# Step sizes of a state-space layer computed in two halves: eight token tiles inside the norm stage ahead of it, eight inside its scan, and a reordered opening of the scan

## The reference, cut to what matters

```python
h = rmsnorm(hidden_states, norm_w)
z, xBC, dt = split(h @ in_proj_w.T)            # 256, 512 and 4 columns
xBC = silu(causal_conv(xBC, 4 taps) + conv_b); x, B, C = split(xBC)
dt = softplus(dt + dt_bias)                    # one step size for each token and head
dA = exp(dt * -exp(A_log))                     # its decay
h_t = h_{t-1} * dA_t + dt_t * B_t x_t          # scan over the tokens, 4 heads
y_t = C_t . h_t + D * x_t;  y = rmsnorm(y * silu(z), w) @ out_proj_w.T
```

## Time and profile before

| | us |
|---|---|
| median of 3 runs (1836.56 to 1837.46) | 1837.18 |
| the profiled execution, whole | 1835.85 |
| its span, from first to last instruction | 1834.1 |
| the state-space stage, first TensorE work to the next stage's | 1427.89 to 1559.38 |
| of it the opening, to the first `scores` | 1427.89 to 1464.30 |

### The profile page before, as it was taken

How to read it: one execution, slowest core, us unless ns; L and a number is a source line. 1 busy time by engine, 2 the same in 40 slices (tenths; PEclk the granted TensorE clock), 3 DMA queues, 4 the chain that set the end, 5 groups by cost and what they waited for, 6 DMA issues and landing times. The chain is left out here.

```text
span 1834.1 us, 25946 instructions
## 1 busy us (share of the span) xinstructions
PE 1683.9 (92%) x10028; PEld 795.2 (43%) x10028; DVE 1263.6 (69%) x1804; ACT 1194.6 (65%) x2436; POOL 182.9 (10%) x171
## 2 busy tenths in 40 slices
PE   6999999999999999749999999999886699699997
PEld 3433333333333333235444444455554466344443
DVE  4888888888888887046888677675375276255555
ACT  4588888888888888735677777777546564333332
POOL 1000000000000000130000000111245000100100
PEclk9899999999999999979899999999988799699999
DMA  1000000000000000010000000000100000212220
GB/s 61 1 1 1 1 1 1 1 1 1 1 1 1 1 1 1 20 28 1 1 1 1 1 1 1 1 1 2 36 1 0 12 1 1 106 60 93 98 84 26
DMA packets 7274, 29.98 MB, mean 16 GB/s; under 512 B 680, under 2 KB 2736, under 8 KB 4848
## 3 DMA queue, kind: packets, MB, share of 16 engines
q1 hardware_dynamic: 7152, 28.33, 4.2%
HBM read 27.15 MB, written 1.18 MB: 15 GB/s over the span
## 5 line engine op out<-in xcount | busy, mean ns | idle before, releaser
L879 DVE TENSOR_REDUCE a_part_max<-a_ps 128x2 f32<-128x1024 f32 x512 | 602.3, 1220 | 87.1 <-PE a_ps L681 86.5
L864 ACT ACTIVATE a_probs<-a_ps 128x512 f32<-128x512 f32 x1024 | 533.2, 613 | 131.0 <-PE a_ps L777 128.6
L879 DVE TENSOR_REDUCE f_part_max<-f_ps 128x2 f32<-128x1024 f32 (+3 forms) x320 | 327.7, 1061 | 121.3 <-PE f_ps L681 65.3
L777 PE MATMUL a_ps<-a_q_shift,a_KA 64*128 64x512 f32 x1024 | 367.7, 448 | 3.8 <-POOL a_q_shift L660 2.6
L864 ACT ACTIVATE f_probs<-f_ps 128x512 f32<-128x512 f32 (+3 forms) x640 | 300.2, 538 | 99.8 <-PE f_ps L781 48.6
L777 PEld LDWEIGHTS a_ps<-a_q_shift,a_KA 64*128 64x128 f32 x1024 | 166.4, 187 | 291.4 <-ACT a_probs L864 275.5
L681 PE MATMUL a_ps<-a_KA,a_q_open 64*128 64x512 f32 x1024 | 277.7, 468 | 4.4 <-DVE a_part_max L879 3.7
L795 PE MATMUL a_psO<-a_probs,a_VA 128*32 128x512 f32 x2048 | 275.6, 610 | 3.9 <-ACT a_probs L864 3.9
L777 PE MATMUL f_ps<-f_q_shift,f_KA 64*128 64x512 f32 (+3 forms) x640 | 224.1, 435 | 4.8 <-POOL f_q_shift L660 2.2
L681 PE MATMUL f_ps<-f_KA,f_q_open 64*128 64x512 f32 (+3 forms) x640 | 170.3, 430 | 5.2 <-DVE f_part_max L879 4.4
L777 PEld LDWEIGHTS f_ps<-f_q_shift,f_KA 64*128 64x128 f32 x640 | 106.3, 188 | 150.2 <-ACT f_probs L864 138.5
(11 more groups left out here) (321 smaller groups left out, 1780.3 us busy)
## 6 DMA issues: line engine op xcount, KB each, us to landing
t_c_all<-c_rows SPq DMA_DIRECT2D x16, 1024.0 KB, 8.0
experts_w<-in_experts SPq DMA_DIRECT2D x1, 3264.0 KB, 10.3
W<-in_weights SPq DMA_DIRECT2D x1, 1574.0 KB, 6.3
out<-X SPq DMA_DIRECT2D x4, 256.0 KB, 6.9
K<-in_consts SPq DMA_DIRECT2D x1, 644.0 KB, 7.0
R<-in_rows SPq DMA_DIRECT2D x1, 530.0 KB, 6.0
W<-in_weights SPq DMA_DIRECT2D x1, 512.0 KB, 6.8
mx_conv_rows<-in_conv_rows SPq DMA_DIRECT2D x1, 512.0 KB, 4.1
```

The source lines that it names most:

```text
L777: mm = pe.matmul(bank(r)[:, lo:512], g.KA[rows, 2 * n + jp, P * s:P * s + P], q_shift[rows, u % 2, jp, lo:512], start=True, stop=not diag)
L864: nc.scalar.activation(probs[:, st % 2, j, lo:512], bank(r)[:, lo:512], ACT.Exp, scale=SCALE).then_inc(ring_read, 1)
L879: dve.tensor_reduce(part_max[:, 4 * q + 2 * jp:4 * q + 2 * jp + 2, c], ps1[:, k % 2, :, 0:b - a], AX_X, ALU.max).then_inc(max_read, 1)
```

## The change

A class `StepSizes` now holds the whole calculation for eight tiles. It is used twice. The first use (`u_`, tiles 0 to 7) is written into the norm stage: `logits` on TensorE after its last `add_scaled`, `sums` between the two last `turn_u`; on VectorE `raw` after the last `mixture`, `one_more` and `step_size` ahead of `stats3(3)`; on ScalarE `exp_raw` and `log` around `apply2(3)`, and `decays` ahead of the last block. There, `scale_u`, the part of `apply3` that makes `U`, is split off and put ahead of `apply3` for the two last blocks. The second use (`mx_`, tiles 8 to 15) is written into the scan: `logits` at chunk 1, `sums` at chunk 5; `raw`, `one_more`, `step_size` at chunks 1, 2, 3; `exp_raw` and `log` in ScalarE's part for block 1, `decays` in that for block 2. `dt`, `a`, `decay` and `Aneg` are now allocated outside the two stages. In the opening, `decays_of(0)` comes ahead of the convolutions, `spread_a(0)` is ScalarE's first work, `exponent(0)` follows the pad copies, and `spread_a(1)` and `(2)` stand ahead of the Silu work.

The diff, cut to its core (`...` marks what is left out):

```diff
+class StepSizes:
...
+    def logits(self, pe, bank):
+        for t in range(8):
+            at = CONV - 1 + P * (self.first + t)
+            mm = pe.matmul(bank[:, MH * t:MH * t + MH], g.UT[:, at:at + P], g.w("mzdt")[:, DI:DI + MH], start=True, stop=True)
...
+    def log(self, act):
+
+        act.wait_ge(self.one_in, 1)
+        act.activation(self.small[:, 2], self.small[:, 1], ACT.Ln).then_inc(self.log_in, 1)
...
@@ norm stage, TensorE
+                pe.wait_ge(ut_sb, 2)
+                sizes.logits(pe, ps[:, 3, :]).then_inc(dt_ps, 1)
                 turn_u(NB - 2)
+                sizes.sums(pe, ps[:, 3, 8 * MH:]).then_inc(sums_ps, 1)
                 turn_u(NB - 1)
@@ norm stage, ScalarE
+                nc.scalar.activation(g.Aneg[:], g.r("alog"), ACT.Exp).then_inc(aneg, 1)
+                sizes.exp_raw(nc.scalar)
                 apply2(NB - 1)
+                sizes.log(nc.scalar)
+                scale_u(NB - 2)
                 apply3(NB - 2)
                 copy_ut(NB - 2)
+                act.wait_ge(sums_ps, 1)
+                sizes.decays(nc.scalar, ps[:, 3, 8 * MH:32 * MH], decays)
+                scale_u(NB - 1)
                 apply3(NB - 1)
                 copy_ut(NB - 1)
@@ norm stage, VectorE
                 mixture(NB - 1)
+                dve.wait_ge(dt_ps, 1)
+                sizes.raw(dve, ps[:, 3, 0:8 * MH])
                 mean3(NB - 2)
                 mean2(NB - 1)
+                sizes.one_more(dve)
+                dve.wait_ge(aneg, 1)
+                sizes.step_size(dve)
                 stats3(NB - 1)
                 mean3(NB - 1)
@@ state-space stage, TensorE
+                    if c == 1:
+                        sizes.logits(pe, s_bank(c)[:, P + DI:])
+                    if c == 5:
+                        sizes.sums(pe, s_bank(c)[:, P + DI + 8 * MH:])
...
@@ state-space stage, ScalarE, within the loop over blocks
+                    if b == 0:
+                        sizes.exp_raw(nc.scalar)
+                        sizes.log(nc.scalar)
+                    if b == 1:
+                        act.wait_ge(sums_in, 1)
+                        sizes.decays(nc.scalar, sums_sb[:], decays)
                     silu_conv(n, 0)
...
@@ state-space stage, VectorE, within the loop over chunks
+                        if c == 1:
+                            sizes.raw(dve, s_bank(c)[:, P + DI:P + DI + 8 * MH])
+                        if c == 5:
+                            dve.tensor_copy(sums_sb[:], s_bank(c)[:, P + DI + 8 * MH:]).then_inc(sums_in, 1)
...
+                        if c == 2:
+                            sizes.one_more(dve)
+                        if c == 3:
+                            sizes.step_size(dve)
```

More of the change, by code:

```diff
@@ L949, in apply_norm, with __init__, sums, then @@
                              bias=nb[:, i:i + 1]).then_inc(done, 1)
+class StepSizes:
+    def __init__(self, g, ctx, pre, half):
+        self.g, self.tok = g, slice(8 * half, 8 * half + 8)
+        self.first = 8 * half
+        self.small = g.sb(ctx, pre + "small", [P, 6, 8, MH])
+        self.steps = Count(g.sem(pre + "dt_step"))
+        self.raw_in, self.raw_exp, self.one_in, self.log_in, self.a_done = (
+            g.sem(pre + x) for x in ("raw", "raw_exp", "one_more", "log", "a"))
+    def logits(self, pe, bank):
+        g = self.g
+        for t in range(8):
+            at = CONV - 1 + P * (self.first + t)
+            mm = pe.matmul(bank[:, MH * t:MH * t + MH], g.UT[:, at:at + P], g.w("mzdt")[:, DI:DI + MH], start=True, stop=True)
+        return mm
+    def sums(self, pe, bank):
+        g = self.g
+        pe.wait_ge(self.a_done, 1)
+        for n, name in enumerate(("upto", "after", "ones")):
+            mm = pe.matmul(bank[:, 8 * MH * n:8 * MH * (n + 1)], g.k(name),
+                           g.a[:, self.tok, :].rearrange("p c h -> p (c h)"), start=True, stop=True)
+        return mm
+    def then(self, dve, ins):
+        dve.wait_ge(self.steps.sem, self.steps.up(ins))
+    def raw(self, dve, src):
+        g, small, dt = self.g, self.small, self.g.dt[:, self.tok, :]
+        self.then(dve, dve.tensor_tensor(dt, src.rearrange("p (c h) -> p c h", h=MH), over_tiles(g.r("dtb"), 8), ALU.add))
+        self.then(dve, dve.tensor_scalar(small[:, 5], dt, -1.0, None, ALU.mult))
+        dve.tensor_tensor(small[:, 0], dt, small[:, 5], ALU.min).then_inc(self.raw_in, 1)
+    def exp_raw(self, act):
+        act.wait_ge(self.raw_in, 1)
+        act.activation(self.small[:, 0], self.small[:, 0], ACT.Exp).then_inc(self.raw_exp, 1)
+    def one_more(self, dve):
+        small, dt = self.small, self.g.dt[:, self.tok, :]
+        dve.wait_ge(self.raw_exp, 1)
+        self.then(dve, dve.tensor_scalar(small[:, 1], small[:, 0], 1.0, None, ALU.add))
+        dve.tensor_scalar(small[:, 3], small[:, 1], -1.0, None, ALU.add).then_inc(self.one_in, 1)
+        dve.wait_ge(self.one_in, 1)
+        self.then(dve, dve.tensor_scalar(small[:, 4], small[:, 3], 0.0, None, ALU.is_equal))
+        self.then(dve, dve.tensor_tensor(small[:, 3], small[:, 3], small[:, 4], ALU.add))
+        self.then(dve, dve.reciprocal(small[:, 5], small[:, 3]))
+        self.then(dve, dve.tensor_scalar(dt, dt, 0.0, None, ALU.max))
+    def log(self, act):
+        act.wait_ge(self.one_in, 1)
+        act.activation(self.small[:, 2], self.small[:, 1], ACT.Ln).then_inc(self.log_in, 1)
+    def step_size(self, dve):
+        g, small, dt = self.g, self.small, self.g.dt[:, self.tok, :]
+        dve.wait_ge(self.log_in, 1)
+        self.then(dve, dve.tensor_tensor(small[:, 2], small[:, 2], small[:, 5], ALU.mult))
+        self.then(dve, dve.tensor_tensor(small[:, 2], small[:, 2], small[:, 4], ALU.add))
+        self.then(dve, dve.tensor_tensor(small[:, 2], small[:, 2], small[:, 0], ALU.mult))
+        self.then(dve, dve.tensor_tensor(dt, dt, small[:, 2], ALU.add))
+        self.then(dve, dve.tensor_scalar(small[:, 3], dt, -1.0, None, ALU.mult))
+        dve.tensor_tensor(g.a[:, self.tok, :], small[:, 3], over_tiles(g.Aneg[:], 8), ALU.mult).then_inc(self.a_done, 1)
+    def decays(self, act, src, done):
+        dst = self.g.decay[:, :, self.tok, :].rearrange("p n c h -> p n (c h)")
+        act.activation(dst, src.rearrange("p (n k) -> p n k", n=3), ACT.Exp).then_inc(done, 1)
@@ L1436, in state_space_stage @@
         rows_in, taps_in, pad_clear = S_("rows_in"), S_("taps"), S_("pad_cleared")
-        dt_ps, dt_step, raw_in, one_in, dt_done = S_("dt_ps"), S_("dt_step"), S_("raw"), S_("one_more"), S_("dt")
-        aneg, raw_exp, log_in, a_done = S_("aneg"), S_("raw_exp"), S_("log"), S_("a")
-        sums_ps, decays = S_("sums_ps"), S_("decays")
+        sums_in, decays = S_("sums_copied"), S_("decays")
         ring_ps, ring_read = S_("ring_filled"), S_("ring_read")
@@ L1556, in outputs @@
                               start=True, stop=True).then_inc(y_ps, 1)
[L1558 to L1561 removed]
                 project(0, COPY_B)
                 project(0, COPY_C)
+                decays_of(0)
                 convolve(0, 0)
                 convolve(0, 1)
[L1566 to L1570 removed]
                 turn_x(0, 0)
@@ L1575, in _ @@
                 turn_b(0)
-                for c in range(4):
+                for c in range(1, 4):
                     decays_of(c)
@@ L1683, in _ @@
                 silu_taps(0, 1)
-                for c in range(2):
-                    spread_a(c)
                 skips(0, 0)
@@ L1690, in _ @@
                 copy_b(0)
-                for c in range(2, 4):
-                    spread_a(c)
-                for c in range(4):
+                spread_a(3)
+                for c in range(1, 4):
                     exponent(c)
```

71 lines of the change are left out of this document (21 added, 50 removed).

## The result

The changed kernel took 1827.78 us, median of 5 runs (1826.86 to 1829.71), against 1837.18 for 5 runs of the kernel before (1836.56 to 1838.82): ratio 0.9948, 95% interval 0.9937 to 0.9959.

What follows compares the result with a forecast made beforehand. The prediction took the path through the scan's opening to bound the kernel, TensorE's step-size products delaying `project` and the convolution; -11.7 + 0.4 + 4.4 + 0.6 = -6.3 us gave 1830.9 us, range 1828.2 to 1835.0.

Steps and rivals of the forecast that it cites:

- The opening: Scan's start, TensorE's first work to the first `scores`: 24.7 us instead of 36.4, a gain of 11.7 (10.0 to 12.6).
- block 0: Scan's first block: second half's products, a stall and later VectorE work cost 4.4 us (1.7 to 6).
- the rest of the scan: Block 1 pays 0.6 us (0 to 0.8) for `sums`, a copy and an exponential; blocks 2 and 3 unchanged.
- thin products: In the scan's first block, TensorE gets 16 more step-size passes ahead of `scores(1)`, costing 1.7 us.
- stall: In the scan's first block, `turn_x(1,0)` waits for ScalarE's Silu queued behind the logarithm: 1.9 us.
- slower, the clock stays half: Rival: TensorE still at half clock at the first `scores`, slowing convolution and first block; 1849 us, chance 0.04.
- The cover is gone: Rival: the scan's first convolution starts late or slow, waiting for `taps` or at half clock; up to 1838 us, chance 0.13.
- Each switch costs more: Rival: ScalarE's two table switches on the path cost another 1.28 us each; 1833.5 us, chance 0.03.
- the median of the runs is 1.33 higher: Whole kernel: profiled execution took 1835.85 us, its successor 1829.6; the median, 1.33 higher, becomes 1837.18 - 6.3 = 1830.9.
- the ends don't fall together: Whole kernel: bounds together give -10.7 to -2.0 us, narrowed to -8.9 to -3.7 for the forecast's own case.
- `step_size` in the norm stage: Six VectorE operations take 1.3 us, starting `stats3(3)` 0.15 late, within a norm-stage cost of 0.4 (0.2 to 1.2).
- the sign that the prediction had named for being wrong: Norm stage: a wait of over 1 us before `stats3(3)` would show the forecast wrong.

Runs made afterwards that it cites:

- e4: Changed kernel with the second half's step-size products issued between `decays_of(2)` and `decays_of(3)`, their follow-up work also earlier: 1824.33 us, ratio 0.9929 to the kernel before.
- e10: Changed kernel with the second half's `step_size` moved behind `values(1,1)` and `decayed(1)` in the scan: ratio 0.9947 to the kernel before.
- e1: The kernel before, with no edit, profiled a second time and timed again: ratio 0.9995 to the kernel before.
- e2: The changed kernel, with no further edit, profiled a second time and timed again: ratio 0.9951 to the kernel before.
- e3: Changed kernel with the opening's order put back as before and the two halves kept: ratio 1.0002 to the kernel before.

## Why the prediction was right and wrong

**Right.** The opening (-12.33 for -11.7), block 0 (+3.93 for +4.4) and the rest of the scan (+0.67 for +0.6), against the execution they were worked out from. Their mechanisms held one by one: `taps` ends the wait at +6.45; ScalarE's copies cost nothing, having ended with the switch before the convolution's first half; the late exponentials set the end; in block 0 thin products, stall and `step_size` are shown by experiments (e4 the first two together, e10 the third). At full clock throughout, block 0 costs 4.3 rather than 3.93, nearer still to the 4.4. That `taps` came on time was in part luck, as said above. The rival "slower, the clock stays half" did not come: the clock was 1.00 when the convolution began. "The cover is gone" came in its small form, 1.36 us idle, already in the sum. "Each switch costs more" fell by its rows.

**Wrong, the base.** The failed step is the line of the sum that takes the profiled execution's 36.4 and 27.2 us for those of before and carries the difference over to the median as it is ("the median of the runs is 1.33 higher"). I knew from the earlier trace rows that the clock was half and then rose during `project`, and asked what a half clock would do to the convolution *after* the change, but not whether it could do the same to the convolution *before*. It usually does: opening + block 0 of 65.6 in two of three profiles, 63.6 in the one I used, and the mean clock of those two in 60 of 94 timed executions. Against e1's rows the region changes by 1.31 - 13.48 + 3.04 + 0.65 = -8.5 us. The last stage adds 0.4 to 2.0, by the table's rows, and the stretch ahead averages out (1404.3 and 1404.2). That is 8.9 to 10.5, where 9.4 and, in e2, 9.0 were measured. The range had bounds for the changed opening only, and none for the old one; with another 2 us below it would have held. Its bounds added up to a gain of 10.7 us, which would have taken in the 9.4, and were drawn in to 8.9 because "the ends don't fall together"; had they been left, it would have held by luck, since none of them is for this cause.

**Wrong, a term.** `step_size` in the norm stage: 0.15 on the path was forecast, from rows of VectorE's small operations with nothing beside them. In the change the first of them meets GpSimd's addition, which stood in the timeline of before at just that time, and costs 0.9 more. `stats3(3)` began 13.13 us after the start of the last `add_scaled` group instead of 12.07, 1.06 late, which meets the sign that the prediction had named for being wrong (over 1 us ahead of `stats3(3)`). 1.31 is over the upper bound of 1.2, which had assumed 0.2 for each operation.

**Underrated.** Without the reordering the halves gain nothing (e3). The reordering alone wasn't run: `decays_of(0)` at that place needs `a`, which before is ready only 15.7 us after the stage's start, so the two belong together. The prediction named `taps` as its limit but counted `decays_of(0)` only as 1.57 us of work moved; it also holds the clock for the convolution (7.1 against 10.0).

**Open.** How the clock's share splits between the opening's parts wasn't tried. Nor was what makes the last stage differ, by 1.3 us among three profiles of before and by more among the variants. Its first 60 us have a granted clock of 0.74 in all three profiles of before and 0.77 in both of the changed kernel; I estimate from that difference up to 1.8 us (0.03 of 60), but what causes it isn't known.

## What to carry to other kernels

Profile the kernel before at least twice ahead of a forecast, cut it into stretches, and take as a term's base the stretch's usual value; where TensorE's granted clock isn't 1.00, put the same uncertainty on the old order as on the new. In this kernel pauses of TensorE of two or three microseconds could cost more than themselves, because work behind them ran at half clock: fill them with work that is needed anyway, or even with work that isn't. Before placing a small VectorE operation with two SBUF inputs, look at what GpSimd does at that time.
